# Layer 0 attention of a gated two-layer block: bias read in place, and another order of copies and transposes in each step

## What is computed

```python
# batch b: 512 latents (from x), 512 media rows (ctx); H = 8 heads of 128
q = layernorm(x) @ Wq + bq                       # 512 x 1024
k, v = split(concat([norm(ctx), norm(x)]) @ Wkv + bkv)   # 1024 keys
sim = (q * 128 ** -0.5) @ k.T                    # per head 512 x 1024
out = softmax(sim) @ v
x = x + tanh(g_xattn[0]) * (out @ Wo + bo)
```

## Time and profile before

| what | value |
|---|---|
| time before, median of 3 runs | 3115.68 us (3115.3 to 3116.95) |
| the profiled execution's own time | 3124.96 us |
| its span | 3123.3 us |
| PE busy / DVE busy / ACT busy / POOL busy | 92% / 72% / 58% / 55% of the span |
| layer 0 attention in the profile | from the start to about 1595 us |
| steps 2 to 62 | 78 to 1560 us, 20 to 27 us each |

### The profile page before, as it was taken

One profiled execution on the slowest core, in us unless ns is written; L12 is line 12 of the kernel. 1 busy time (PEld: TensorE's weight loads), 2 busy tenths in 40 slices (PEclk: granted clock), 3 DMA queues, 4 the chain that ended last, 5 costly groups with the idle time before them and its releaser, 6 DMA issues. The chain is left out here.

```text
span 3123.3 us, 46820 instructions
## 1 busy us (share of the span) xinstructions
PE 2865.7 (92%) x17032; PEld 2286.6 (73%) x17032; DVE 2241.8 (72%) x3546; ACT 1799.2 (58%) x2774; POOL 1706.6 (55%) x1054
## 2 busy tenths in 40 slices
PE   6999999999999999999959958999999976999999
PEld 5777877778777877877849944555555445999999
DVE  6777777777777777777745547777777635578887
ACT  3555555555545555455525526888888853366665
POOL 3543544435444354443334426888887743568886
PEclk9999999999999999999979978999999988999999
DMA  5654333333333433333245634444433122368885
GB/s 150 211 180 127 98 119 91 112 124 96 119 96 110 126 92 118 98 106 114 81 150 202 218 106 140 117 122 123 123 116 95 49 87 97 106 184 236 226 236 147
DMA packets 295880, 409.73 MB, mean 131 GB/s; under 512 B 30323, under 2 KB 216850, under 8 KB 295664
## 3 DMA queue, kind: packets, MB, share of 16 engines
q1 hardware_dynamic: 274864, 375.28, 37.9%
q0 software_dynamic: 18656, 29.00, 4.8%
q10 hardware_dynamic: 2144, 2.62, 0.3%
HBM read 259.51 MB, written 149.04 MB: 131 GB/s over the span
## 5 line engine op out<-in xcount | busy, mean ns | idle before, releaser
L1789 POOL TENSOR_TENSOR c_pT_lo<-c_prob,c_pT_hi 128x1024 fp32r<-128x1024 f32 x192 | 456.4, 2384 | 115.6 <-ACT c_pT_hi L1872 111.6
L482 ACT ACTIVATE a_prob<-a_scores,a_neg_max 128x1024 f32<-128x1024 f32 x256 | 285.7, 1116 | 396.9 <-DVE a_neg_max L606 396.9
L403 POOL TENSOR_TENSOR a_pT_lo<-a_turned,a_pT_hi 128x1024 fp32r<-128x1024 f32 x64 | 152.7, 2386 | 656.1 <-ACT a_pT_hi L474 656.1
L606 DVE TENSOR_REDUCE a_neg_max<-a_scores 128x1 f32<-128x1024 f32 x256 | 309.9, 1211 | 90.5 <-PE a_scores L36 87.5
L1984 DVE TENSOR_REDUCE c_neg_max<-c_max 128x2 f32<-128x1024 f32 x248 | 302.2, 1219 | 72.6 <-PE c_max L2217 71.5
L1866 ACT ACTIVATE c_prob<-c_scores 128x1024 f32<-128x1024 f32 x256 | 261.3, 1021 | 72.5 <-PE c_scores L2228 67.9
L34 PE MATMUL m_h<-m_rT_hi,m_w_hi 128*128 128x256 f32 x880 | 253.8, 288 | 2.3 <-DVE m_rT_lo L2718 1.9
L35 PE MATMUL m_h<-m_rT_lo,m_w_hi 128*128 128x256 f32 x880 | 248.9, 283 | 1.0 <-issue 1.0
L36 PE MATMUL m_h<-m_rT_hi,m_w_lo 128*128 128x256 f32 x880 | 248.6, 282 | 0.7 <-issue 0.7
L34 PE MATMUL a_pj<-a_pT_hi,a_v_hi 128*128 128x512 f32 x512 | 208.0, 406 | 43.9 <-DVE a_qT_lo L538 40.6
L2613 POOL TENSOR_TENSOR m_w_lo<-m_w_in,m_w_hi 128x1024 fp32r<-128x1024 f32 x80 | 201.6, 2520 | 59.0 <-ACT m_w_hi L2661 58.6
(11 more groups left out here) (354 smaller groups left out, 9182.4 us busy)
## 6 DMA issues: line engine op xcount, KB each, us to landing
m_w_in<-L_ffn_w_in SPq DMA_DIRECT2D x117, 512.0 KB
blocks_dram<-a_turned SPq DMA_DIRECT2D x64, 512.0 KB, 2.6
a_turned<-blocks_dram SPq DMA_DIRECT2D x256, 128.0 KB, 2.9
blocks_dram<-a_prob SPq DMA_DIRECT2D x64, 512.0 KB, 3.1
a_prob<-blocks_dram SPq DMA_DIRECT2D x256, 128.0 KB, 3.0
e_w_in<-L_ffn_w_in SPq DMA_DIRECT2D x32, 1024.0 KB, 7.6
qk_dram<-c_stage SPq DMA_DIRECT2D x64, 256.0 KB
c_q_rows<-qk_dram SPq DMA_DIRECT2D x32, 512.0 KB, 5.1
```

Of the source, the lines that this page charges most:

```text
L403: g.tensor_tensor(by_query(pT[1], t), from_blocks(staged[t]), by_query(pT[0], t).bitcast(F32), ALU.subtract).then_inc(turned_lo, 1)
L482: a(prob[:, qt, :], ps_s[:, qt % 2, :], ACT.Exp, bias=neg_max[:, qt:qt + 1], accum_out=row_sum[:, par, qt:qt + 1]).then_inc(exp_done, 1)
L606: ve.tensor_reduce(neg_max[:, qt:qt + 1], ps_s[:, qt % 2, :], AX.X, ALU.max, negate=True).then_inc(max_done, 1)
L1789: g.tensor_tensor(flat(pT[1][:, kt - 1]), flat(prob[:, kt]), flat(pT[0][:, kt - 1]).bitcast(F32), ALU.subtract).then_inc(lo_pool, 1)
```

## The change

The order of PE's own items does not change in any step. What changes: `qk_bias` and its copy go, the bias columns are read from `bias`; `tr0` moves from behind `turn3` to behind `scores1` and `tr1` from behind `scores2` to in front of it; `hi0` moves to directly behind `fin1` (save in step 7 mod 8), in even steps `hi1` moves from behind `turn2` to behind `v1`; routing and statistics that DVE did after `scores1` now follow `tr0`, and those after `scores3` now follow `scores2` (save `route_locate` and `route_keep`).

```diff
             if par == 0:
-                steps = "scores0 turn3 tr0 qk0 qk1 scores1 fin0 scores2 tr1 fin1 scores3 qk2 v0 hi0 v1 v2 out0 turn2 hi1 v3 out1"
+                steps = "scores0 turn3 qk0 qk1 scores1 tr0 fin0 tr1 scores2 fin1 hi0 scores3 qk2 v0 v1 hi1 v2 out0 turn2 v3 out1"
             elif hp == 1 and b:
-                steps = "scores0 turn3 tr0 qk0 zt0 scores1 fin0 scores2 tr1 fin1 zt1 scores3 lg0 qk1 hi0 qk2 out0 turn2 out1 hi1"
+                steps = "scores0 turn3 qk0 zt0 scores1 tr0 fin0 tr1 scores2 fin1 hi0 zt1 scores3 lg0 qk1 qk2 out0 turn2 hi1 out1"
             elif hp == 2 and b:
-                steps = "scores0 turn3 tr0 qk0 scores1 fin0 scores2 tr1 fin1 cn0 scores3 qk1 hi0 qk2 out0 turn2 out1 hi1"
+                steps = "scores0 turn3 qk0 scores1 tr0 fin0 tr1 scores2 fin1 hi0 cn0 scores3 qk1 qk2 out0 turn2 hi1 out1"
             elif hp < 3:
-                steps = "scores0 turn3 tr0 qk0 scores1 fin0 scores2 tr1 fin1 scores3 qk1 hi0 qk2 out0 turn2 out1 hi1"
+                steps = "scores0 turn3 qk0 scores1 tr0 fin0 tr1 scores2 fin1 hi0 scores3 qk1 qk2 out0 turn2 hi1 out1"
             elif b < B - 1:
-                steps = "scores0 turn3 tr0 pro2 scores1 pro3 scores2 pro0 tr1 fin0 scores3 fin1 qk0 pro1 hi0 qk2 out0 qk1 turn2 out1 hi1"
+                steps = "scores0 turn3 pro2 scores1 pro3 scores2 pro0 tr0 fin0 tr1 scores3 fin1 qk0 pro1 hi0 qk2 out0 qk1 turn2 hi1 out1"
             else:
-                steps = "scores0 turn3 tr0 scores1 fin0 scores2 tr1 fin1 scores3 hi0 out0 turn2 out1 hi1"
+                steps = "scores0 turn3 scores1 tr0 fin0 tr1 scores2 fin1 hi0 scores3 out0 turn2 hi1 out1"
...
-                if kind == "qk" and j == 0:
-                    act.wait_ge(qk_bias_set, n + 2)
+                if use == ("qk", 0) and n < 0:
+                    act.wait_ge(set_up, 2)
...
-                    a(qk_dst(0, j, 1 - par), src, ACT.Identity, bias=qk_bias[:, 1 - par, i:i + 1]).then_inc(hi_done, 1)
+                    a(qk_dst(0, j, 1 - par), src, ACT.Identity, bias=bias[:, (n + 1) % H0, i:i + 1]).then_inc(hi_done, 1)
...
-                    lo(qk_dst(1, j, 1 - par), src, qk_dst(0, j, 1 - par), qk_bias[:, 1 - par, i:i + 1]).then_inc(pj_out, 1)
+                    lo(qk_dst(1, j, 1 - par), src, qk_dst(0, j, 1 - par), bias[:, (n + 1) % H0, i:i + 1]).then_inc(pj_out, 1)
...
-            def set_qk_bias(h, par):
-                ve.tensor_copy(qk_bias[:, par, :], pick(bias[:], h)[:, 0:2]).then_inc(qk_bias_set, 1)
...
-                if n < 8 * B - 1:
-                    set_qk_bias((n + 1) % H0, 1 - par)
...
-                    if after == ("scores", 1):
+                    if after == ("tr", 0):
                         if at == (0, 0) and b or at == (0, 1) and not b:
...
-                    elif after == ("scores", 3):
+                    elif after == ("scores", 2):
                         if at == (0, 1) and not b:
...
-                        elif at == (3, 1) and b:
+                    elif after == ("scores", 3):
+                        if at == (3, 1) and b:
```

More of the change, by code:

```diff
@@ L82, in layer0_attention @@
         bias = sb("bias", [P, H0, 3])
-        qk_bias = sb("qk_bias", [P, 2, 2])
         tbo = sb("tbo", [P, D])
@@ L126, in layer0_attention @@
         set_up = sem("set_up")
-        qk_bias_set = sem("qk_bias_set")
         x_load = sem("x_load")
@@ L681, in _ @@
             dve.wait_ge(set_up, 2)
-            set_qk_bias(0, 0)
             rescale(0, (0, 1, 2, 3))
```

## The result

The changed kernel takes 3182.7 us (median of 4 runs, 3181.2 to 3183.9) against 3115.5 (3115.2 to 3117.0), a ratio of 1.021, interval 1.020 to 1.023. The forecast was 3160 with a range of 3105 to 3195.

What follows compares the result with a forecast made beforehand. PE sets the pace, busy 1415 of 1517 us, plus its waits. Seven batches of +5.4 give 38, the last batch and end 6: +44 on the median of 3115.7 gives 3160, range 3105 to 3195.

Steps and rivals of the forecast that it cites:

- Copy and tr0 ahead of qT_lo: DVE's queue ahead of qT_lo: either item gone would nearly suffice; almost all of PE's 47.2 us of waits go.
- hi0's wait: ACT behind fin1 stands still about 2 us in nearly every step for block 0's DRAM trip, 7.5 us from write issue.
- steps 1 and 5: Odd steps mod 8: hi0 delays the key copies and out0, loss 2.4 against about 1.4; taken as +0.6 each.
- Steps 0 and 2: Even steps mod 8: hi0 and hi1 delay v1 and v3, loss 3.0 to 3.7 against 2.5; taken as +0.7 each.
- Steps 4 and 6: Mod 8: POOL's normalise delays the split, loads and hi1's trip; hi1 ahead of v2 delays v3, +2.1 each.
- none of this starts earlier: In step 28, the loads, write and read-back behind POOL's split were said to start no earlier after the change.
- rival C: The clock falls after new idle stretches of about 2.9 us: 14 steps lose 3.4 more each, 3208; chance 0.09.
- the 44 of the sum: Forecast loss over the whole kernel: 38 us in seven batches and 6 in the last batch and at the end.
- Rival A: The qT_lo gain is kept and ACT's waits do not come, given trips of at most 5.0: 3060; chance 0.13.
- Rival B: ACT's slack takes up the waits on hi0; only hi1 in steps 4 and 6 costs: 3113; chance 0.13.
- Step 7: Mod 8: tr0 moves behind the low part of pro on DVE, PE's 1.42 wait goes; gain 1.4.
- Step 3: Mod 8: qT_lo's wait ahead of fin0 goes, one of like size ahead of lg0 comes; 0.

Runs made afterwards that it cites:

- bias alone: Kernel before with only the bias copy removed and the bias columns read in place: 3075.4 us, ratio 0.987.
- all hi back: Changed kernel with hi0 and hi1 of all steps at their old places; the rest of the change stays: 3080.7 us, ratio 0.988.
- the first two experiments: Changed kernel with hi1 behind turn2 again in even steps, 3097.2 us; changed kernel with hi0 and hi1 of every step at their old places, 3080.7 us.
- the run with hi1 back: Changed kernel with hi1 behind turn2 again in the even steps, hi0 staying behind fin1: 3097.2 us, ratio 0.993.
- the combination: Kernel before with bias read in place, hi0 behind qk2 in steps 1, 3, 5, and tr0, tr1 later in step 7 mod 8: 3063.6 us, ratio 0.982.
- hi0 and hi1 moved, alone: Kernel before with only hi0 and hi1 at the places they have in the changed kernel: 3156.6 us, ratio 1.012.

## Why the prediction was right, and which terms were off

**Copy and tr0 ahead of qT_lo.** Right: PE's waits for it fell from 47.2 to 6.3, and bias alone, with tr0 in its old place, took out 37 of them. That either would nearly do is shown for the copy: all hi back, with tr0 moved as well, is no faster than bias alone. tr0 moved with the copy left in place was not run.

**hi0's wait.** Right in kind: ACT waits for block 0 in 58 steps. The trip was too long in my sum. In step 24 the write is issued at 653.45 and ACT starts at 660.43, 7.0 us later and not 7.5 (7.4 in step 0). hi0 in steps 1 and 5 was put at +0.6 each, measured -0.1 and -0.5. Part of this is in the working: the odd step's own numbers, low part at 13.1 and place of out0 at 11.2, give a loss of 1.9, not the 2.1 written. The rest is probably the shorter trip. Steps 0 and 2, put at +0.7, measured +0.6 and +0.3. hi0 alone costs 16 us by the first two experiments. PE's waits for `kT_lo` came to 52.2, where above 60 was forecast.

**Steps 4 and 6.** The mechanism is the one described (SP's loads wait for POOL's split, hi1 now stands ahead of v2), and all of the loss of batches 1 to 6 is there; the term of +2.1 each was mis-sized: +3.0 and +5.9. Two things were left out. First, "none of this starts earlier" was taken for "nor later". In step 29 hi1 waits 1.6 for its own trip, POOL's low part and `normalise` follow it, and the split of step 30 ends 17.2 us behind `scores0` (808.02 against 790.82), where it had ended 15.5 behind in step 28 of the kernel before. That puts the write at 809.0, 18.2 behind it. Second, the clock, which I had as rival C.

**Rival C** came true in part. PE's busy time rose by 21 us. It was priced at 48 for fourteen steps. In the changed kernel's trace half speed follows 12 of the 13 waits of 2.5 us and more for `v_lo`, the 4.42 in step 0, and two shorter waits (1.87 and 0.53). Without the 21 the layer's 62 would be about 41 (an estimate), near the 44 of the sum. That is partly luck, for the terms erred both ways: the first batch lost 17 and not 5.4, since the waits of its steps 0, 4 and 6 are longer; the last gave back 1.5 and did not lose 4, and the 2 us behind it did not come (from `scores0` of step 63 to PE's first work behind the layer it is 39.3 us before and 39.2 after). The rule of the Trainium skill ("TensorE: Matmul & The Clock Gate", Part 1), that the clock drops to 1.2 GHz after an idle stretch, agrees with the windows above: 4.46 us idle, then 0.56. The last section has drops that follow much shorter waits.

**Rival A** asked for a trip of 5.0; it takes 7.0 to 7.4. **Rival B** held that hi0's wait would be taken up: in the run with hi1 back, where it can be seen alone, it costs some 16 us, which is small against its 102 us of waits on ACT. B was nearer on hi0 than my sum, and wrong on hi1.

**Step 7** gained 1.1, forecast 1.4. **Step 3** gained 0.4, forecast 0.

What is shown: the place of hi1 (85 to 107 us), the order on SP (66), the order on POOL (52), the bias copy (41, alone). What is argued only: the split of the loss into waits and clock, which rests on PE's busy time and not on a run that holds the clock up, and how hi0's 16 us divide between ACT's wait and DVE's work that GpSimd lengthens. The new places of tr and DVE's order cost 5 by themselves (all hi back against bias alone) and 43 with hi early.

## What to carry to other kernels

On an engine that works in order, do not put an instruction that waits for a transfer ahead of one that frees a buffer for the bottleneck engine; put it behind, however early its own result might be had. Before moving a wait forward, follow the transfer back through every queue that issues it: in step 30 of the changed kernel the block was ready at 803.8, but its write was issued at 809.0, behind loads that waited for GpSimd's split. Parts of a reordering do not add: with one engine's chain as the bound, a saving elsewhere is worth less or nothing (41 us or 17 for the same edit). And an engine off the critical path can move work onto it: with hi0 earlier GpSimd started earlier too, and small DVE instructions that then ran beside it took 1.5 us instead of 0.2.

## What the runs showed of the hardware

**The clock can fall without a long idle stretch.** In the run with all hi back, step 27 has a wait of only 0.53 us, then 16 products of 16 columns; the matmuls behind them run slow (timeline of PE, that run):

```profile
690.95 1.96 PE L1270 MATMUL a_pj<-r_wg,a_zero 128*128 128x16 f32 x16 [0.53 <-DVE a_zero L574]
692.75 0.67 PE L34 MATMUL a_pj<-a_kvT_hi,a_wqk_hi 128*128 128x512 f32 x1
693.22 0.63 PE L35 MATMUL a_pj<-a_kvT_lo,a_wqk_hi 128*128 128x512 f32 x1
```

The window from 693 to 700 has a granted clock of 0.77 in that run with PE busy all the time, and from 672 to 690 it had been 1.00 with PE busy all the time too. It explains why step 3 takes 22.7 us in some batches and 24.0 in others. In the kernel before, the same products followed a wait of 0.19 and the clock stayed full in all seven batches. But the length of the wait does not decide it alone. With 0.53 the clock fell in 5 of 6 batches with all hi back, in 1 of 6 in the changed kernel and in 22 of 42 over the seven kernels that have this wait; with 0.19 it fell in 3 of 42, two of them in the combination, where the window from 1050 to 1057 has 0.76:

```profile
1050.67 1.96 PE L1269 MATMUL a_pj<-r_wg,a_zero 128*128 128x16 f32 x16 [0.19 <-DVE a_zero L574]
```

What decides between such cases these runs do not show. Waits near 2 us are as mixed: with all hi back, those of 1.96, 2.36, 1.89 and 1.89 for `oT_lo` in step 6 were each followed by half speed (0.76 from 764 to 771), a fifth of 1.90 was not, nor were two of 1.80 and 1.87 in the run with hi1 back.

**Small DVE instructions take long beside GpSimd.** In step 30 of the changed kernel the routing's four sums, 64 bytes a partition each, take 2.78 us together (timeline of DVE):

```profile
799.90 2.78 DVE L1201 TENSOR_TENSOR r_sums<-r_sums,r_counts 128x16 f32<-128x16 f32 x4
802.60 1.24 DVE L596 STREAM_TRANSPOSE a_prob<-a_prob 128x1024 f32<-128x1024 f32 x1
```

The timeline of GpSimd over the same stretch:

```profile
800.51 1.92 POOL L387 TENSOR_TENSOR a_y<-a_y,a_rstd 128x1024 f32<-128x1024 f32 x1
```

GpSimd's operation ends at 802.43, the sums at 802.68. In the last batch there is no `normalise`, and GpSimd does nothing beside the same four sums (DVE, step 62 of the changed kernel):

```profile
1604.21 0.76 DVE L1201 TENSOR_TENSOR r_sums<-r_sums,r_counts 128x16 f32<-128x16 f32 x4
```

In the run with the split ahead of `normalise`, where only GpSimd's order was edited, they take 3.52 in step 30 and end at 773.72, again 0.25 behind an operation of GpSimd (771.05 to 773.47). In the view by tile one of the 32 sums takes 134 to 1757 ns in the changed kernel, and 130 to 2307 in the run with all hi back, for the same shape. The bias copy of two columns, 1.65 us in the earlier trace rows, ended there at 661.19, 0.03 behind a GpSimd operation that had begun at 658.78 and ended at 661.16. And in "hi0 and hi1 moved, alone" DVE's `r_first` went from 0.19 to 1.53 once GpSimd worked beside it. So a small DVE instruction can last until GpSimd's current one ends. That it goes with GpSimd's work is shown by these pairs of the same instruction; what the two engines contend for, no run here shows.
